# Attention with a quantised gate: norm, quantisation, x turns and coefficient moved, three steps of lookahead in place of two

## The reference, cut to what matters

```
xn = layernorm(x)                                 # no affine part
qkv = xn @ Wqkv.T + b      # 16 q heads, 8 k heads of 128, 4 value heads of 256
p1, p2 = causal softmax of the two maps of each of 8 head pairs (two pairs share k and v)
o = (p1 - lam * p2) @ v    # lam: one scalar of four vectors
o = rms-normalised o (256 wide) * subln_w * const
s = o @ out_w.T + out_b
a, w = mxfp4 quantise-dequantise of xn and of weight, blocks of 32
g = silu(a @ w.T + bias)
out = x + s * g
```

## Time and profile before

| what | value |
|---|---|
| time, median of 3 runs | 1780.74 us (1776.7 to 1782.26) |
| profiled execution, its own time | 1780.72 us |
| its span, first to last instruction | 1778.5 us |
| mean granted TensorE clock | 0.963 |
| prologue, up to batch 0's step 0 | 134.8 us |
| DMA engines, mean share | 29.9% for the queue of SyncE |

### The profile page before, as it was taken

How to read it: one execution, slowest core, us unless ns; L and a number is a source line. 1 busy time by engine, 2 the same in 40 slices (tenths; PEclk the granted TensorE clock), 3 DMA queues, 4 the chain that set the end, 5 groups by cost and what they waited for, 6 DMA issues and landing times.

```text
span 1778.5 us, 29365 instructions
## 1 busy us (share of the span) xinstructions
PE 1569.9 (88%) x9425; PEld 921.1 (52%) x9425; DVE 1237.2 (70%) x3213; ACT 874.0 (49%) x2514; POOL 737.3 (41%) x1442
## 2 busy tenths in 40 slices
PE   2657898998889988999889988899988998899998
PEld 2334554555554555555554555545555555555554
DVE  4668888548884588746885488845887478854782
ACT  4554555335653356434553356534564355533561
POOL 2214563236542464324642364424643246323243
PEclk9888999999899999999999998999989999899999
DMA  7302223332233222332233223322233222322342
GB/s 266 95 1 68 49 45 63 76 61 56 55 83 61 55 50 55 81 73 50 49 59 78 66 51 57 84 57 59 47 62 75 72 50 54 54 55 65 60 77 69
DMA packets 331980, 117.55 MB, mean 66 GB/s; under 512 B 312978, under 2 KB 313524, under 8 KB 331828
## 3 DMA queue, kind: packets, MB, share of 16 engines
q1 hardware_dynamic: 331828, 115.70, 29.9%
HBM read 31.74 MB, written 8.39 MB: 23 GB/s over the span
## 4 chain that ended last, share of the span: by engine, by line
PE 36%; DVE 28%; POOL 13%; issue 12%; ACT 10%; DMA 1%; POOLq 0%; SPq 0%; ACTq 0%; DVEq 0%
PE ps L456 11%; PE ps L458 11%; PE ps L457 11%; DVE ps L935 5%; DVE qkv L891 4%; DVE pp L947 4%; DVE ph L953 4%; ACT qkv L635 3%; ACT ph L670 3%; DVE coef L944 2%; POOL norm L1138 2%; POOL gate L1112 2%; ACT pp L662 2%; POOL qkv L1098 2%; POOL v L1110 1%
## 5 line engine op out<-in xcount | busy, mean ns | idle before, releaser
L456 PE MATMUL ps<-xT,wqkv 128*128 128x512 f16 x768 | 297.5, 387 | 26.4 <-DVE qkv L891 24.6
L670 ACT ACTIVATE ph<-pp,small 128x128 f16<-128x128 f32 (+3 forms) x256 | 143.3, 560 | 320.3 <-DVE pp L947 319.3
L457 PE MATMUL ps<-xT,wqkv 128*128 128x512 f16 x768 | 296.1, 386 | 0.0
L458 PE MATMUL ps<-xT,wqkv 128*128 128x512 f16 x768 | 295.7, 385 | 0.0
L935 DVE CUSTOM_DVE_ANT_0 ps<-ps,mask,ssc 128x384 f32<-128x384 f32 (+3 forms) x512 | 281.9, 551 | 6.1 <-PE ps L520 6.1
L891 DVE SCALAR_TENSOR_TENSOR qkv<-ps,bsc,qkv 128x512 f16<-128x512 f32 x192 | 142.8, 747 | 140.4 <-ACT qkv L635 140.4
L674 ACT ACTIVATE junk<-ps 128x256 bf16<-128x256 f32 x256 | 97.1, 379 | 261.2 <-PE ps L458 261.1
L456 PE MATMUL ps<-qkv,pT 128*128 128x256 f16 x640 | 182.0, 284 | 37.8 <-DMA pT<-ph 36.6
L1136 POOL TENSOR_TENSOR norm<-norm,sumsq 128x1 f32<-128x1 f32 x256 | 49.5, 193 | 389.8 <-ACT junk L674 389.6
L953 DVE SCALAR_TENSOR_TENSOR ph<-pp,small,ph 128x128 f16<-128x128 f32 (+3 forms) x256 | 174.1, 680 | 43.1 <-ACT ph L670 30.6
L456 PE MATMUL ps<-wout,heads 128*128 128x512 f16 x512 | 194.1, 379 | 3.6 <-DVE small L921 3.3
(11 more groups left out here) (146 smaller groups left out, 3441.9 us busy)
## 6 DMA issues: line engine op xcount, KB each, us to landing
xin<-in_L_attn_hidden_states SPq DMA_DIRECT2D x8, 1024.0 KB, 5.6
xres<-in_L_attn_hidden_states SPq DMA_DIRECT2D x32, 256.0 KB, 2.8
out_x<-res SPq DMA_DIRECT2D x32, 256.0 KB, 2.3
qkv<-in_L_attn_Wqkv_w SPq DMA_DIRECT2D x8, 512.0 KB, 9.6
heads<-in_L_attn_Wqkv_w SPq DMA_DIRECT2D x8, 512.0 KB, 11.8
pT<-ph SPq DMA_TRANSPOSE x256, 2.7
heads<-on SPq DMA_TRANSPOSE x256, 2.5
qkv<-in_L_attn_out_w SPq DMA_DIRECT2D x4, 512.0 KB, 4.2
```

The lines of the kernel that those rows point to most:

```text
L456: mm(out, ah, bh, start=start and j == 0, stop=False)
L457: mm(out, ah, bl, start=False, stop=False)
L458: last = mm(out, al, bh, start=False, stop=stop and j == n - 1)
L670: run(ph[:, u, 0:w], pp[:, 0:w], ACT.Copy, scale=sigma).then_inc(ph_hi, 1)
```

## The change

- `AHEAD = 3`: TensorE issues `scores(n + 3)` in step n, VectorE works on `combine(n + 2)` and `maxima(n + 3)`, ScalarE on `p_hi(n + 2)` and `exps(n + 3)`; SyncE turns n + 2 first in its step, ahead of loads and stores. pT has three buffers; ph has one (`PH = 4 - AHEAD`), so `p_hi(n)` waits until the turn of n - 1 has landed. The scores still have two double banks, now freed by `p_lo` (n - 2).
- `combine` is one VectorE operation, in PSUM; `p_hi` and `p_lo` read PSUM. Reciprocal (a power of -1) and coefficient are on GpSimd in `eps_of`.
- xT, aT and wT fills are gone. x is split in SBUF (ScalarE `x_hi`, VectorE `x_lo`, steps 15 to 19) and turned by DMA on SyncE, two 128 x 1024 float16 tiles in each of steps 21 and 22; aq is turned by DMA in steps 9 and 10; ffn is in steps 10 to 13.
- x is quantised in steps 1 to 4 of its own batch, batch 0 too; the gate's weights in steps 5 to 8 of batch 0. The next x is loaded at step 5 and its norm is in step 7: statistics on VectorE, the root on GpSimd, one scaling on ScalarE instead of two operations of GpSimd.
- After an "out" in step n - 1, VectorE takes its fill ahead of the maxima; SyncE leaves out the turn of o in odd steps below 8 and makes two in the next.
- The prologue turns x by DMA ahead of the weight loads 4 to 15, and ScalarE splits x between the squares 3 and 4.

```diff
+AHEAD = 3
+PH = 4 - AHEAD
+QUANT_AT = {(s + ds, slot): [(k + a, op) for a, op in ops] for s, k in ((1, 0), (3, 2)) for ds, slot, ops in (
+    (0, "maxima", [(0, 0), (0, 1), (0, 2), (0, 3)]),
+    (0, "projected", [(0, 4), (0, 5), (1, 0), (1, 1), (1, 2), (1, 3)]),
+    (1, "projected", [(1, 4), (1, 5)]))}
+PROJ_AT = (0, 0, 1, 2, 3, 4, 6, 7)
-        at = range(STEPS) if g < 3 else (0, 0, 1, 1, 2, 3, 4, 5)
+        at = (None, PROJ_AT, PROJ_AT[:6] + (7, 8), (0, 1, 1, 2, 3, 3, 4, 5))[g]
...
+X_SPLIT = {15: 0, 17: 1, 18: 2, 19: 3}
+X_TURN = {21: (0, 1), 22: (2, 3)}
...
-                wait(sp, pv_done, n - 1)
+                wait(sp, pv_done, n - AHEAD + 1)
...
+                if n + AHEAD - 1 < NSTEPS:
+                    transpose_p(n + AHEAD - 1)
...
+                for k in X_TURN.get(s, ()) if b + 1 < B else ():
+                    sp.wait_ge(fill_done, fill_of("v", b, G - 1, k // 2) + 1)
+                    transpose_x((b + 1) * NT + k)
...
-                wait(pe, comb_done, n - 1)
+                wait(pe, ph_lo, n - 1)
...
             def p_hi(n):
                 act.wait_ge(comb_done, n + 1)
-                wait(act, pT_done[u], 16 * (n // 2))
-                run(ph[:, u, 0:w], pp[:, 0:w], ACT.Copy, scale=sigma).then_inc(ph_hi, 1)
+                if n >= PH:
+                    act.wait_ge(pT_done[(n - PH) % AHEAD], 16 * ((n - PH) // AHEAD + 1))
+                run(ph[:, n % PH, 0:w], sc_ps[u][:, 1, 0:w], ACT.Copy, scale=sigma).then_inc(ph_hi, 1)
...
             def combine(n):
-                dve.wait_ge(exp_done, 2 * n + 2)
-                nc.vector.reciprocal(recip[:], l2).then_inc(recip_done, 1)
-                dve.wait_ge(recip_done, n + 1)
-                stt(out=coef[:, u:u + 1], in0=recip[:], scalar=neglam, in1=l1, op0=ALU.mult, op1=ALU.mult)\
-                    .then_inc(coef_done, 1)
                 dve.wait_ge(coef_done, n + 1)
-                stt(out=pp[:, 0:w], in0=sc_ps[u][:, 1, 0:w], scalar=coef[:, u:u + 1], in1=pp[:, 0:w],
+                stt(out=sc_ps[u][:, 1, 0:w], in0=sc_ps[u][:, 1, 0:w], scalar=coef[:, u:u + 1], in1=pp[:, 0:w],
...
             for n in range(NSTEPS):
                 if n:
                     norm_of(n - 1)
...
+                if n + AHEAD < NSTEPS:
+                    eps_of(n + AHEAD)
+                for f in PLAN[n - 1] if n else ():
+                    if f.kind == "ffn":
+                        gating(f)
+                    elif f.kind == "out" or f.kind == "last" and LAST_PIECES[f.j][f.g][1] == OC:
+                        finish(f)
...
-                if n + 2 < NSTEPS:
-                    eps_of(n + 2)
```

More of the change, by code:

```diff
@@ L74, in schedule @@
             steps[2 * k + 1].append(("out", 0, k))
[L76 to L82, removed]
+        steps[FFN_STEP + k].append(("ffn", 0, k))
     if has_next:
         last = 3 * STEPS
-        for k in range(NT):
-            steps[last - 2 + k // 2].append(("xT", 0, k))
-        for s, (kind, j) in enumerate(PROJ):
+        for s, (kind, j) in zip(PROJ_AT, PROJ):
             steps[last + s].append((kind, 0, j))
@@ L95, in schedule @@
     return steps
[L98 to L113, removed]
+PROLOGUE = [(kind, 0, j) for kind, j in PROJ]
+X_SPLIT = {15: 0, 17: 1, 18: 2, 19: 3}
+X_TURN = {21: (0, 1), 22: (2, 3)}
+Fill = namedtuple("Fill", "kind g j n hi v ffn gate out bank prev")
 def plan():
     n = hi = v = ffn = 0
+    used, held, bank = [-1, -1], None, 1
     rows = []
@@ L127, in plan @@
                 out = 4 * b + (j if kind == "last" else j - NT)
-                row.append(Fill(kind, g, j, n, hi, v, ffn, gate, out))
+                bank = held if kind == "last" and g else 1 - (bank if held is None else held)
+                row.append(Fill(kind, g, j, n, hi, v, ffn, gate, out, bank, used[bank]))
+                if kind == "last":
+                    held = bank if LAST_PIECES[j][g][1] < OC else None
+                used[bank] = n
                 n += 1
-                hi += kind in ("q", "k", "xT")
+                hi += kind in ("q", "k")
                 v += kind == "v"
@@ L133, in plan @@
             rows.append(row)
-    return rows[0], rows[1:], n
-FIRST, PLAN, FILLS = plan()
+    end = []
+    for k in (NT - 2, NT - 1):
+        bank = 1 - bank
+        end.append(Fill("out", 0, k, n, 0, 0, 0, 0, (B - 1) * NT + k, bank, used[bank]))
+        used[bank] = n
+        n += 1
+    return rows[0], rows[1:], end
+FIRST, PLAN, END = plan()
 assert len(FIRST) % 2 == 0
-END = [Fill("out", 0, k, FILLS + k - (NT - 2), 0, 0, 0, 0, (B - 1) * NT + k) for k in (NT - 2, NT - 1)]
 NSTEPS = B * NS
@@ L164, in setup_order @@
 def setup_order():
-    order = [("w", n) for n in range(8)] + [("fill", i) for i in range(NT)]
-    i = NT
+    order = [("w", n) for n in range(8)]
+    i = 0
     for n in range(8, WB):
@@ L294, in build @@
         ph_lo = sem("ph_lo")
[L295 removed]
+        pT_done = [sem(f"pT_done{u}") for u in range(AHEAD)]
         pv_done = sem("pv_done")
@@ L555, in _ @@
                     pe.wait_ge(fill_free, len(PROLOGUE) - 2)
-                    scores(1)
+                    for a in range(1, AHEAD):
+                        scores(a)
                     continue
@@ L981, in _ @@
                 elif kind == "ahead":
-                    combine(0)
-                    maxima(1, 1)
-                    p_lo(0)
-                    maxima(1, 0)
+                    for a in range(1, AHEAD):
+                        combine(a - 1)
+                        maxima(a, 1)
+                        p_lo(a - 1)
+                        maxima(a, 0)
                 elif kind == "w":
@@ L1022, in _ @@
+                if n + AHEAD < NSTEPS and not late:
+                    maxima(n + AHEAD, 1)
+                if n + AHEAD - 1 < NSTEPS:
+                    p_lo(n + AHEAD - 1)
+                for f in late:
+                    fill(f)
+                if n + AHEAD < NSTEPS:
+                    if late:
+                        maxima(n + AHEAD, 1)
+                    maxima(n + AHEAD, 0)
+                prepare(b, s, "maxima")
                 if n:
                     normalised_lo(n - 1)
-                prepare_some(b, s, 1)
```

381 lines of the change are left out of this document (197 added, 184 removed).

## The result

The changed kernel takes 1822.95 us (median of 4 runs, 1817.45 to 1824.86), the kernel before 1781.08 us beside it (4 runs, 1776.7 to 1782.26). The ratio is 1.0235, 95% interval 1.0207 to 1.0263: slower, where 1700 us was forecast and 1775 was the end of the range.

What follows compares the result with a forecast made beforehand. TensorE bounds a third of a batch, the softmax chain around a loaded VectorE the rest; 1780.7 - 72 (six middle batches) + 3 (batch 0) - 6 (prologue) - 6 (last batch) = 1700 us, range 1640 to 1775.

Steps and rivals of the forecast that it cites:

- the sum for a middle batch: TensorE work 180, narrow-step loop 4.5, step 24 waiting 5, clock 3, small waits 2.5: 195 us, -12 a batch.
- point 3: Coefficient on GpSimd: VectorE's softmax cycle some 5.1 us for 512 columns; one step of slack covers 0.5 us delay, not 2.
- rival C: GpSimd late with the coefficient behind gating and rounding: 204 us a batch, about 1760 us; chance 0.17.
- Point 4: Lookahead of three, one split-weights buffer: turned-weights waits go, but its loop costs some 4.5 us a batch in narrow steps.
- Rival D: The single split-weights buffer bounds every step: 6.8 us a step, 218 us a batch, about 1850 us; chance 0.12.
- Point 5: SyncE's queue: x turns in steps 21 and 22 make TensorE wait 5 us around step 24, plus 3 us of clock.
- Point 6: Batch 0: VectorE's added quantisation, norm and rounding waits cost +14 us in the first eight steps, later steps return 11: +3.
- Point 7: Prologue: VectorE's wait for GpSimd's rounding goes, against later x splits and a third score of 1.5 us: -6 us.
- Point 8: Last batch: ffn leaves its thin final steps, the rest as elsewhere, tail unchanged: -6 us.
- Points 1 and 2: TensorE loses its turns, -4 us a batch; VectorE sheds work, quantisation hides under the outs, bank waits nearly go.

Runs made afterwards that it cites:

- after: The changed kernel itself, with the whole change, against the kernel before; 1822.9 us, ratio 1.0235.
- e1: Against after, GpSimd does the gating of the step before ahead of the next reciprocal and coefficient, not behind them; 1780.5 us, ratio 1.0011.
- f2: e1 with two buffers of split weights instead of one, still three steps of lookahead; 1746.6 us, ratio 0.9818.
- g1: f3 with the turn of the last x tile moved from step 22 to 21, so two and two; 1718.7 us, ratio 0.9669.
- f3: f2 with the x turns one step earlier, two tiles in step 20, one each in 21 and 22; 1725.5 us, ratio 0.9688.
- g3: f3 with reciprocal and coefficient moved back from GpSimd to VectorE; 1766.9 us, ratio 0.9936.
- g2: f3 with batch 0's norm of the next x moved from step 7 to steps 9 to 12, one tile each; 1732.2 us, ratio 0.9738.
- h1: g1 with batch 0's norm of the next x moved from step 7 to step 9, all four tiles; 1719.2 us, ratio 0.9663.

## Why the prediction was wrong, point by point

**Where the 123 us lie.** In the profiled executions the six middle batches are 12 us each above the forecast's 195 (72 us), batch 0 is 20 above it (+23 where +3 was forecast), the last batch 18 (+12 for -6), the prologue 7 (+1 for -6). That is 117 us; the other 6 are that after's profiled execution was its fastest.

**The step that failed is the sum for a middle batch**, 180 + 4.5 + 5 + 3 + 2.5. The 180 stands: with the forecast's 0.216 us for 512 columns, step by step, it is 179.7. The 15 us on top of it are 27.3 (mean of batches 1 to 6, each step's time less its work): 12.8 in steps 13 to 15, 9.7 in steps 22 to 24, 3.8 in steps 29 and 30. What the edits took out of them, against the sum's terms:

| loss in a middle batch | in the sum | by the runs |
|---|---|---|
| circle through gating and tanh | no term | 3.6 (after to e1) |
| one split buffer | 4.5 | 5.3 (e1 to f2) |
| x turns in the queue, and the clock behind them | 5 + 3 | 3.4 (f2 to g1) |
| all that is left | 2.5 | 14.9 (in g1) |

The last row is the largest miss. In g1 it lies in steps 13 to 15 (4.8), 22 to 24 (4.8) and 29 and 30 (4.7). For the last pair g1's trace shows what it is, VectorE's low halves in batch 2 and TensorE in step 30:

```profile
701.98 0.75 DVE L981 SCALAR_TENSOR_TENSOR ph<-ps,small,ph 128x512 f16<-128x512 f32 x1
...
707.05 0.75 DVE L981 SCALAR_TENSOR_TENSOR ph<-ps,small,ph 128x512 f16<-128x512 f32 x1 [0.44 <-ACT ph L689]
...
707.95 0.26 PE L544 MATMUL ps<-qkv 128*128 128x128 f16 x1 [2.87 <-DVE ph L981]
```

The two low halves are 5.07 us apart, and the scores wait 2.87 us for the second. That is the chain's own cycle, which point 3 of the forecast had worked out rightly as 5.1 us. It was then held against TensorE's 4.9 us for a wide step with a fill, and got no term. But step 29 has no fill: steps 29 and 30 are 5.5 us of work and take 10.2, two cycles. In steps 13 to 15 and 22 to 24 of g1 TensorE waits for a fill bank (step 13, 1.1 us a batch), for low halves of the weights (1.0, 1.8 and 0.9 us in steps 14, 15 and 23) and for the low half of o (1.3 us in step 23). What these wait for in turn was not taken apart and no edit tried it; that part stays open.

From after to the best kernel it is 1822.9 us, less 42 (circle through gating), less 34 (single split buffer), less 28 (x turns): 1718.7, each the difference of two rows of the table.

**Point 3, the coefficient on GpSimd.** It had gating in its right place, behind the coefficient of its own step and ahead of the next one, and asked only what gating delays: rival C. It did not ask what delays gating, and who waits for it. That is not the softmax chain but tanh, which writes the same buffer and has the next exponentials queued behind it; for this circle the sum had nothing, and it cost 42 us. Rival C had the place and a total near the measured one (204 a batch, 1760 us), by another mechanism: combining does wait for the coefficient in after (95.0 us, 91 places), but with gating first these waits stay (103.5 us) and the 42 us come back all the same. Its cure, tried on f3 (g3), was the wrong one. The product's cost was also mis-sized: 0.37 us on average, not 0.2. By lines of after:

```profile
L1161 POOL TENSOR_TENSOR recip<-psum_l,small 128x1 f32<-128x1 f32 x256 | 140.3, 548 | 546.3 <-ACT pp L681 546.3
...
L1163 POOL TENSOR_SCALAR coef<-recip,psum_l,small 128x1 f32<-128x1 f32 x256 | 95.6, 373 | 26.8
```

Of the rule of the GPSIMD Engine Reference of the Trainium skill (section 4.1 Engine selection), that elementwise work belongs on VectorE: for the reciprocal alone it agrees (548 ns, against 153 in the earlier trace rows), for the coefficient there is no difference (373 against 374), and for the kernel g3 speaks against it: the slower engine was the better place by 41 us.

**Point 4, one split buffer**, was right in its mechanism and near in size: 5.3 us a middle batch (203.4 to 198.1) for 4.5, 3.3 in batch 0, 34 us in all. Of the 64 turns of 512 columns in after the median takes 3.27 us to land, as was put in. But 18 of them take over 4 us (5 of 64 in the kernel before), above all the one of item 15: in e1's batch 2 the turns of items 14 and 15, issued at 642.68 and 648.57, took 3.2 and 4.8 us. Rival D (the pace everywhere, 218 a batch) is false: wide steps such as 28 run at TensorE's pace, 4.87 us, in both. The X-Bar Transpose section of the Advanced Engine Details and Errata page of the Trainium skill says that turns are as fast as plain transfers; here 256 KB turned take 3.27 us at the median against 2.7 us plain (residual loads, median), and up to 5.3.

**Point 5, the queue.** The place was right, the size half of what was put in. In after step 24 takes 11.0 us for 6.2 of work, and moving the x turns gave 28 us over seven batches, 4 a batch (3.4 in the traces of the middle ones), for 5 + 3. The clock was forecast at 0.98 and is 0.935: in the windows of batch 2 above, steps 8 to 15 alone lose 48.0 x 0.11 = 5.3 us to it, which the forecast did not have, and steps 16 to 31 41.6 x 0.03 + 42.9 x 0.05 = 3.4 us. These lie within the 27.3, behind the waits, and are not a loss on top.

**Point 6, batch 0, was wrong by 20 us.** Steps 1 to 7 take 53.5 us against 45.6 before, +8 where +14 was forecast for the first eight; but steps 8 and 9 take 11.99 and 16.70 us, where middle batches take 6.16 and 3.89, and before they took 8.49 and 4.97. The windows of batch 0, steps 1 to 7 and 8 to 15:

```profile
139.20:192.70 53.50, 32.70 (x195) 19.74 (x193) 38.14 (x88) 18.40 (x56) 30.00 (x42) 0.84 0.28 58
192.70:260.40 67.70, 44.46 (x221) 23.63 (x223) 42.06 (x103) 30.25 (x85) 38.98 (x69) 0.80 0.29 50
```

The point summed VectorE's work over steps 0 to 7 and forgot that the weights' last share is in step 8 and that the norm of step 7 puts four scalings on ScalarE ahead of the next high half. g2 and h1 show 7 us of it in that norm. The rest was not taken apart further; what stands there beside the norm are VectorE's waits for rounding (12.1 us in batch 0, of which part is covered) and the clock of 0.80 to 0.84.

**Point 7, prologue.** The first turn of p is issued at 127.27 us, 6.1 us earlier than before (133.42), which is the 6 us forecast. But step 0 ends 1.1 us later (139.18 against 138.05): nothing was left of it. The third score and its chain, put at 1.5 us, stand ahead, and a second fill in step 0. In the three kernels with two steps of lookahead step 0 ends at 135.5 to 136.2 us, in those with three at 137.3 to 139.9.

**Point 8, last batch.** Forecast -6, measured +12.3 (229.1 against 216.8). It counted that ffn leaves the thin final steps, and not what ffn costs where it goes: steps 8 to 15, which had none before, take 46.8 us and not 36.8. 7.4 of these 10 us are the same two losses (41.2 in e1, 39.4 in f2). The steps behind gave nothing back (16 to 31: 80.4 us against 77.6).

**Points 1 and 2** hold for what they name: 75.3 us for steps 0 to 7, and the low half of 512 columns takes 751 ns for 1041. The bank waits did not go, though, but moved to the ffn (19.2 us; 8 once gating is first). That g1's middle batch is 194.7 us, where 195 was forecast for this kernel, is luck: g1 has neither the one buffer nor most of the queue's loss, which the 195 had counted.

## What to carry to other kernels

When an edit moves operations between engines, draw the circle for every buffer with one copy: who waits for its release, what is queued in order behind that wait, and whether that leads back to the release. Busy times don't show such circles; a wait without a DMA or a slow engine behind it, on a lightly loaded engine, does. And when two loops run through the same steps, undoing one shows less than it costs (8 to 14 us became 34 us): try them together before calling a part harmless. Last, a cycle that has been worked out belongs in the sum of every step whose own work is shorter than it (here 5.1 us against steps 29 and 30), not only against the widest.

## What the runs showed that was not expected

- A DMA turn's issue takes nearly the same time whatever it moves: 1.17 us for a 128-column p, 1.23 us for a 512-column one, 1.28 us for x. Two a step (p and o) are 2.5 us, more than a narrow step without a fill takes at best (2.24 us, step 22 of g1), so the queue has no room there for anything else.
- Turns of the same size take 3.05 to 5.3 us to land, and the slow ones come at fixed places: of the 18 over 4 us among the 64 of 512 columns in after, seven are of item 15 and six of item 22. The cause stays open.
- The granted clock falls with short waits: behind 1.84 us of idling (f3, with three waits of 0.9 to 1.3 us ahead of it) seven matmuls of 512 columns ran 0.38 to 0.43 us apart in place of 0.216.
- The power on GpSimd for the reciprocal takes 0.548 us, and the norm's, 0.640 us in the earlier trace rows, takes 0.558 in after, with its operands in other places; whether that is the reason was not tried.
